# The projection of the last two image groups issued one unit earlier, apart from its bf16 remainders

## The reference

```python
x = conv1x1(x, W_in); x = depthwise3x3(x, W_dw) + b_dw      # 96 channels
x_proxy = conv1x1(x, W_xd)                                   # 16 channels
ws, Ls, Us, Ds = (conv1x1(x_proxy, W) for W in (W_w, W_l, W_u, W_d))
xs = [x, x_t, flip(x), flip(x_t)]                            # 4 directions d
Gl, Gm, Gr = ws[:, :nd], ws[:, nd:2*nd], ws[:, 2*nd:]
s = abs(Gl) + abs(Gm) + abs(Gr) + 1e-7;  Gl, Gm, Gr = Gl/s, Gm/s, Gr/s
# chunks of 8 columns, per step:
h = l * x + gl * h_up + gm * h + gr * h_down
out = h * Us + xs * Ds;  y = sum over d of w_m[d] * out[d]
y = layernorm2d(y);  y = grn(y);  return conv1x1(y, W_out)
```

## Time and profile before

| | |
|---|---|
| median of 3 runs | 947.7 us (946.01 to 948.82) |
| profiled execution, its time | 948.81 us |
| profiled execution, span | 946.7 us, mean granted TensorE clock 0.856 |
| PE busy | 765.9 us (81%) |
| DVE busy | 799.2 us (84%) |
| ACT busy | 575.0 us (61%) |
| POOL busy | 236.0 us (25%) |

### The profile page before, as it was taken

One profiled execution on the slowest core, in us unless ns is written; L12 is line 12 of the kernel. 1 busy time (PEld: TensorE's weight loads), 2 busy tenths in 40 slices (PEclk: granted clock), 3 DMA queues, 4 the chain that ended last, 5 costly groups with the idle time before them and its releaser, 6 DMA issues.

```text
span 946.7 us, 20432 instructions
## 1 busy us (share of the span) xinstructions
PE 765.9 (81%) x7926; PEld 507.4 (54%) x7926; DVE 799.2 (84%) x2011; ACT 575.0 (61%) x857; POOL 236.0 (25%) x270
## 2 busy tenths in 40 slices
PE   2699999999999999999999969799578667533346
PEld 1467877787788778877777753384122111100013
DVE  7899999999889999989999944744629999899984
ACT  1387777778778777787767733214456665555133
POOL 6222222222222222222222221572201221212101
PEclk9799999999999999999999978788786655555667
DMA  8200000000000000002000000100003674667501
GB/s 235 67 2 3 2 2 2 2 2 2 2 1 2 2 1 3 1 2 109 1 2 2 2 1 7 45 1 0 1 1 68 122 134 81 131 127 137 104 0 33
DMA packets 11622, 34.13 MB, mean 36 GB/s; under 512 B 1879, under 2 KB 4359, under 8 KB 11271
## 3 DMA queue, kind: packets, MB, share of 16 engines
q0 software_dynamic: 5904, 21.24, 11.7%
q1 hardware_dynamic: 5623, 11.60, 4.0%
HBM read 10.81 MB, written 0.79 MB: 12 GB/s over the span
## 4 chain that ended last, share of the span: by engine, by line
PE 53%; DVE 32%; ACT 6%; issue 5%; POOL 1%; DMA 1%; POOLq 0%; DVEq 0%; ACTq 0%
PE narrow L1470 7%; DVE prod L982 4%; PE wide L1391 4%; PE scores_a L1451 4%; DVE prod L990 3%; PE scores_b L1451 3%; PE last L1549 3%; PE wide L1535 3%; DVE mx L608 3%; PE narrow L1500 2%; PE last L1522 2%; PE narrow L1403 2%; DVE v L602 2%; PE scores_a L1440 2%; DVE hst L994 2%
## 5 line engine op out<-in xcount | busy, mean ns | idle before, releaser
L379 POOL TENSOR_TENSOR stb<-stb,neg_half 128x4 f32<-128x4 f32 x48 | 48.4, 1008 | 329.4 <-DVE stb L673 329.4
L1470 PEld LDWEIGHTS narrow<-v,pt 128*64 128x64 f32 x2304 | 82.2, 142 | 16.5 <-issue 16.5
L1108 ACT ACTIVATE d<-d 128x768 f32<-128x768 f32 x96 | 80.7, 841 | 16.3 <-DVE d L620 15.6
L1470 PE MATMUL narrow<-v,pt 128*64 128x54 f32 x2304 | 88.5, 229 | 0.0
L1714 PE MATMUL scores_b<-xb,gates_w 128*32 128x512 bf16 x192 | 27.1, 581 | 60.3 <-DVE yo L1002 52.5
L1124 ACT ACTIVATE ga<-wide 128x512 f32<-128x512 f32 x48 | 28.7, 598 | 67.4 <-PE wide L1535 67.4
L602 DVE COPY v<-narrow 64x96 f32<-64x96 f32 x192 | 49.0, 255 | 13.5 <-PE narrow L1403 10.8
L1108 ACT ACT_TABLE_LOAD x46 | 59.0, 1283 | 0.8
L1132 ACT ACT_TABLE_LOAD x46 | 59.0, 1283 | 0.8
L1391 PE MATMUL wide<-xa,wts 113*120 113x256 f32 x192 | 55.9, 415 | 0.8 <-ACT xa L1084 0.8
L374 POOL TENSOR_TENSOR sta<-sta,neg_half 128x4 f32<-128x4 f32 x48 | 53.0, 1104 | 12.6 <-DVE sta L561 12.6
(11 more groups left out here) (348 smaller groups left out, 2223.2 us busy)
## 6 DMA issues: line engine op xcount, KB each, us to landing
gsum<-mag POOLq DMA_DIRECT2D x14, 512.0 KB, 4.6
ysum<-yo POOLq DMA_DIRECT2D x7, 768.0 KB, 5.6
ysum<-xd POOLq DMA_DIRECT2D x6, 768.0 KB, 5.8
gsum<-mag POOLq DMA_DIRECT2D x14, 256.0 KB, 4.7
wts<-in_wpack SPq DMA_DIRECT2D x6, 442.0 KB, 6.4
sed_w<-in_sed_in SPq DMA_DIRECT2D x1, 2304.0 KB, 8.0
graw<-in_gates_in SPq DMA_DIRECT2D x1, 1152.0 KB, 4.9
x_all<-in_x_tok SPq DMA_DIRECT2D x8, 96.0 KB, 3.0
```

The source lines that it names most:

```text
L379: pool.tensor_tensor(st[n % 2].stb[:, 1], st[n % 2].stb[:, 0], neg_half[:, 0:TILES], ALU.pow).then_inc(rstd2, 1)
L1108: act.activation(d, d, ACT.Exp).then_inc(p_ready[u], 1)
L1470: op = pe.matmul(y_ps[64 * b:64 * b + 64, q * VO:(q + 1) * VO], t.pt[:, q, h, 64 * b:64 * b + 64], t.v[:, q, b, h * VO:(h + 1) * VO], star ...
```

## The change

The two subtractions and their waits leave `project_px` for a function of their own, `remainders_px`. For groups 0 to 3 and for 4 and 5 it is called right behind the projection. For groups 6 and 7 the projection is called in unit 2, behind the remainders of 4 and 5, and the remainders where both were before, behind in_gates(3).

```diff
                         if g == G - 1:
                             op.then_inc(px_done, 1)
+
+            def remainders_px(cs):
+
                 for c in cs:
                     pe.wait_ge(px_hi, c + 1)
                     pe.matmul(B8[PX_BANK[c]][:], minus[:], xb[:, c, :], start=False, stop=True, skip_group_check=True).then_inc(px_rest, 1)
...
             project_px(range(4))
+            remainders_px(range(4))
             gates(0)
...
                 if u == 3:
-                    project_px((6, 7))
+                    remainders_px((6, 7))
                     gates(4)
                 out_gates(u)
                 if u == 2:
                     project_px((4, 5))
+                    remainders_px((4, 5))
+                    project_px((6, 7))
                 elif u < 6:
                     gates(u + 2, (0,))
```

## The result

Over 20 executions each, the changed kernel has a median of 945.75 us and the kernel before 951.53 us; the ratio is 0.9949, interval [0.9936, 0.9963]: 0.51% faster, 4.9 us with 3.5 to 6.1 as bounds. The profiled execution has a span of 942.9 us at a mean clock of 0.861 (before: 946.7 us, 0.856).

The account below looks back on a forecast made before the run. DVE was taken to bound the gate scan, with one 3.64 us wait in unit 4. The terms 0 + 0 - 3.64 + 0 + 0 gave -3.6 us from a median of 947.7: 944.1 us, range 942.4 to 946.2.

Parts of the forecast that it names:

- What bounds the scan, and the one gap: Gate scan, units 1 to 7: DVE runs without idle time except one 3.64 us wait before L966 in unit 4.
- The start and length of the moved projection, the delay of the `in` gates: PE, before unit 3's `in` gates: projection starts about 778.7, lasts 5.28 us, delays gates by 0, at most 0.2 us.
- The remainders without a wait for ACT, 6.06 us earlier: PE in unit 3: ACT's rounding done at 786.2, so remainders of groups 6 and 7 start at 787.9, not 793.96.
- The DMA term: Unit 4's magnitude accumulations, now close behind unit 3's `xd` transfer: 9.64 to 9.9 us to first logarithm, 12.93 at worst.
- The term itself, 3.64 us: DVE before L966 in unit 4: the wait closes whole, with 2.4 us to spare, a gain of 3.64 us.
- The tail: After the units: TensorE's clock rise may shift the end by 1 us up or down; taken as 0.
- The step that failed: Whole kernel: the 3.6 us gain was subtracted from the shown runs' median of 947.7 us, giving 944.1 us.
- Half won: Unit 4: the moved chain meets the `xd` transfer or the guess is otherwise late; gain 2.8 us, 944.9 us; chance 0.12.
- The gap isn't PE's: Unit 4: something that doesn't move holds the gates, so the reorder does nothing, 947.7 us; chance 0.08.
- Slower: Unit 3: `in` gates wait behind the moved projection; 2.0 us slower, 949.7 us; chance 0.05.

Follow-up runs that it names:

- early1: Changed kernel plus one step of unused f32 matmuls (1.7 us) before the moved projection; medians 945.72 and 944.43 us, ratios 0.995 and 0.9957 to the kernel before.
- early3: Changed kernel plus three steps of unused f32 matmuls (5.1 us) before the moved projection; median 949.88 us, ratio 1.0001 to the kernel before.
- late2: Changed kernel plus two pairs of unused f32 matmuls between remainders of groups 6 and 7 and unit 4's gates; median 947.39 us, 0.9976 to the kernel before.
- late7: Changed kernel plus seven pairs of unused f32 matmuls between remainders of groups 6 and 7 and unit 4's gates; median 952.76 us, 1.0043 to the kernel before.

## Why the prediction was right and where it was wrong

**What bounds the scan, and the one gap:** right. All three traces of the kernel before have it, 3.62 to 3.64 us.

**The start and length of the moved projection, the delay of the `in` gates:** right. The changed trace lies 0.26 us earlier from before the diff's first line; with that taken off, 778.7 came out at 778.8, and the `in` gates' 784.12 at 784.19, 0.07 later, against a cover of 0.56. Early1 and early3 showed that this cover is real and what lies beyond it. What the sum had not seen is that it holds for one of two clocks. Its "12 matmuls in six pairs" are six matmuls of two rows each, and its "six f32 matmuls" in the tail are three; the lengths, taken from rows, were not touched by that.

**The remainders without a wait for ACT, 6.06 us earlier:** right, 6.17 us (793.96 against 787.53+0.26); the guess had 2.43 us to spare (2.4 forecast).

**The DMA term:** right at its near end. From the first issue to the first logarithm it took 806.37-796.65 = 9.72 us (9.64 to 9.9 forecast). The `xd` transfer, issued 5.17 us ahead, is listed with 7.3 us to landing (5.7 in the kernel before), so it was still under way when the first accumulation was issued; its bytes were nearly all moved (109 GB/s in 796 to 797 us, 12 in 797 to 798). The interleaving of transfers that the Trainium skill states ("DMA: Bandwidth & Descriptors", "Issuing engines are not separate DMA queues") cost the accumulations next to nothing here: the same time is 9.72 and 9.65 us in the two traces of the changed kernel, 9.64 to 9.66 in the three before. What held the landing of `xd` back is not shown, and no engine is seen to wait for it.

**The term itself, 3.64 us:** right in the scan (3.68 between the first traces), and within the interval of the measured ratio.

**The tail:** the forecast's 0 was 0.15 us, within its bound of 1. Over all traces it takes 38.7 to 40.3 us from L1010 to the end. It is longest (39.9 to 40.3) in four traces, and in all four the clock's second rise came late: the six rows on `narrow` took 5.44 us, where they took 4.17 in the first trace of the kernel before. Its second trace is one of the four; the granted clock was 0.50 in 926 to 930 us and 1.00 from 932 on (PE's timeline):

```profile
926.04 5.44 PE L1831 MATMUL narrow<-ysum,l3w 128*112 128x512 f32 x6
931.28 3.05 PE L1831 MATMUL last<-ysum,l3w 128*112 128x512 f32 x6
```

**The step that failed** is the last one of the sum: "The runs shown have the median 947.7 [...] so the forecast is 947.7 - 3.6". A median of three executions was taken as the level, and its error entered the forecast's own range only within some 1 us to either side, from three runs that spread over 2.8 us. The runs showed a level 3.8 us higher in the first 20 executions (951.53) and 2.3 higher in the median of all 144 (950.0); the same code takes 942.1 to 954.7 us. The traces show where: ahead of the scan, by 5 us between the first two of the kernel before, along with the granted clock at 600 to 650 us. No row of the prediction covered that part. The size of the gain failed only in the medians, and by the same spread: the first 20 against 20 lie 5.8 us apart by their medians and 4.9 by the ratio, all executions 3.8 +- 0.8 in the mean, the traces 3.7. That 945.75 lay within 1.7 us of the forecast is luck: a level too low by 3.8 and a distance too small by 2.2 cancelled for the most part. No second gain was found: the stretch of the scan, which is free of that spread, has none, and the same kind of spread shows between identical kernels (1.0023). That the change has no effect of its own on how the part ahead of the scan falls out was not tested by a run; its code and order are the same there, and L926 comes at 706.27, 701.17 and 708.49 before and at 706.00 and 705.69 after.

**The rivals.** *Half won* needed accumulations slowed down by the transfer; they took 9.72 us, not 12.93. *The gap isn't PE's* fell with late2 and late7. *Slower* was named at the right place with the right point: 4.5 us of wait at 5.1 us of added work.

## What to carry to other kernels

Where one engine is the bound and the list of its waits has a single line, that line is the whole prize; moving work of a waiting engine out of the chain behind it is worth the smaller of the shift and the wait, and what is left of the shift (2.43 us here) is a cover that later edits can use. Price a moved block by what stands behind it in its queue: here DVE had 0.5 us of cover there and the change used 0.07; beyond it each us costs one (4.5 us of wait at 5.1 us of added work). And take the level of a forecast from more than three executions, or state the forecast as a difference: a stretch between two marks in the trace repeated to 0.1 us where whole executions differed by 10.

## What the runs showed of the hardware that was not expected

The chain ahead of DVE's unit 3 has two lengths. The six steps of the projection of groups 4 and 5 were 0.85 us apart in the two traces of the changed kernel and 0.43 us apart in one trace of early1 and in the second of the kernel before, although the same matmuls stood in front of them. What decided between the two is not shown. In the window 765 to 770 us the granted clock was 0.50 (1.2 GHz) in the changed kernel's first trace and 1.00 (2.4 GHz) in that of early1. The same is seen ahead of the scan (0.69 against 1.00 at 630 to 640 us). The lower level can hold through steady work: in the trace of late7 PE went through the added f32 matmuls without idle time from 790.80 to 803.05, and the granted clock was 0.50 in each window of 4 us from 778 to 806. The Trainium skill ("TensorE: Matmul & The Clock Gate", Part 1) says that the place of the transition differs from run to run of one kernel; the traces agree. Here the part ahead of the scan differs by 8 us over the thirteen traces, in the two groups by the clock at 600 to 650 us that are told above, and the tail by 1.6, while the scan, which DVE bounds, differs by 0.1 between traces of the kernel before.
